# A decoder layer on one core: in cross attention ScalarE copies first and VectorE scales the normalised rows; in the experts VectorE makes the down weights' low parts

## What is computed

```python
x = _layernorm(x + attn(x))                        # 16 heads, decayed linear attention
x = _layernorm(x + xattn(x, ctx_1024, ctx_1024))   # 16 heads of 16, 77 keys per sequence, softmax
# experts: xf is x as 4096 rows
probs = softmax(xf @ router_w.T); keep the top 2 and renormalise
g = xf @ gate_w[e] + gate_b[e]; u = xf @ up_w[e] + up_b[e]
expert_out = (silu(g) * u) @ down_w[e] + down_b[e]
y = sum_e probs[e] * expert_out[e]
x = _layernorm(x + y)
```

## Time and profile before

| | |
|---|---|
| median of 3 runs | 1626.9 us (1623.96 to 1629.72) |
| profiled execution | 1613.4 us, span 1611.6 us |
| TensorE busy | 1337.4 us (83%) |
| VectorE, ScalarE, GpSimd busy | 52%, 55%, 50% |
| granted clock of TensorE | 0.917 in the mean |

### The profile page before, as it was taken

One profiled execution on the slowest core, in us unless ns is written; L12 is line 12 of the kernel. 1 busy time (PEld: TensorE's weight loads), 2 busy tenths in 40 slices (PEclk: granted clock), 3 DMA queues, 4 the chain that ended last, 5 costly groups with the idle time before them and its releaser, 6 DMA issues. The chain is left out here.

```text
span 1611.6 us, 30998 instructions
## 1 busy us (share of the span) xinstructions
PE 1337.4 (83%) x10439; PEld 1125.3 (70%) x10439; DVE 841.4 (52%) x1783; ACT 892.4 (55%) x2002; POOL 808.8 (50%) x847
## 2 busy tenths in 40 slices
PE   5999999999999999996877777842699999998500
PEld 4788888888888888885655555522588888888500
DVE  3344444544444444452666566549445544556466
ACT  4677777777777777774255556520345544555200
POOL 2244444444444444454466767611475666667375
PEclk9999999999999999998899999965699999999755
DMA  3300000000000000001223223202254454456154
GB/s 124 74 14 21 21 14 21 21 21 21 15 21 21 21 14 21 15 15 36 69 57 94 75 69 100 63 27 82 72 186 151 143 166 157 153 171 177 52 147 143
DMA packets 123556, 116.42 MB, mean 72 GB/s; under 512 B 42242, under 2 KB 104298, under 8 KB 123434
## 3 DMA queue, kind: packets, MB, share of 16 engines
q1 hardware_dynamic: 116618, 96.23, 19.3%
q0 software_dynamic: 6816, 18.62, 4.3%
HBM read 83.93 MB, written 24.07 MB: 67 GB/s over the span
## 5 line engine op out<-in xcount | busy, mean ns | idle before, releaser
L290 POOL TENSOR_SCALAR_AFFINE_SELECT a_decay<-a_decay 128x256 f32<-128x256 f32 x256 | 113.7, 448 | 260.5 <-ACT a_decay L370 260.5
L493 DVE TENSOR_TENSOR a_probs<-a_ps_s,a_decay 128x384 f32<-128x384 f32 x256 | 131.5, 552 | 164.6 <-PE a_ps_o L668 152.9
L299 POOL TENSOR_TENSOR a_key_sum<-a_probs 128x256 f32<-128x256 f32 x128 | 94.5, 738 | 170.2 <-DVE a_probs L493 159.1
L333 ACT ACTIVATE a_qk_exp<-a_ps_qk 128x512 f32<-128x512 f32 x128 | 76.5, 598 | 136.7 <-PE a_ps_qk L574 129.7
L574 PE MATMUL a_ps_qk<-a_xT_hi,a_w_hi 128*128 128x256 f32 x512 | 144.6, 282 | 3.6 <-ACT a_qk_relu L334 3.6
L486 DVE SCALAR_TENSOR_TENSOR a_qk<-a_qk_exp,a_qk_relu 128x512 f32<-128x512 f32 x128 | 89.3, 698 | 106.9 <-ACT a_qk_relu L334 106.9
L574 PE MATMUL a_ps_qk<-a_xT_lo,a_w_hi 128*128 128x256 f32 x512 | 143.5, 280 | 0.0
L574 PE MATMUL a_ps_qk<-a_xT_hi,a_w_lo 128*128 128x256 f32 x512 | 143.4, 280 | 0.0
L649 PE MATMUL a_ps_s<-a_qk 64*128 64x256 f32 (+1 forms) x1024 | 132.2, 338 | 0.6 <-DVE a_probs L493 0.2
L368 ACT ACTIVATE a_decay<-a_ps_c,a_c_now 128x256 f32<-128x256 f32 x256 | 124.4, 486 | 2.3 <-PE a_ps_c L639 1.4
L956 POOL TENSOR_TENSOR b_probs<-b_probs,b_top 128x1232 f32<-128x1232 f32 x32 | 72.6, 2270 | 103.6 <-DVE b_top L1124 103.6
(11 more groups left out here) (283 smaller groups left out, 4129.4 us busy)
## 6 DMA issues: line engine op xcount, KB each, us to landing
e_gu_raw<-in_L_ffn_gate_w SPq DMA_DIRECT2D x23, 512.0 KB, 3.7
e_gu_raw<-in_L_ffn_up_w SPq DMA_DIRECT2D x23, 512.0 KB, 5.2
e_dn_raw<-in_L_ffn_down_w SPq DMA_DIRECT2D x23, 512.0 KB, 6.7
y_sorted<-e_y_out SPq DMA_DIRECT2D x16, 512.0 KB, 2.9
a_x_in<-in_x SPq DMA_DIRECT2D x16, 256.0 KB, 2.7
a_x_res<-in_x SPq DMA_DIRECT2D x16, 256.0 KB, 2.7
x_rows<-a_x SPq DMA_DIRECT2D x16, 256.0 KB, 2.1
b_x_in<-x_rows SPq DMA_DIRECT2D x16, 256.0 KB
```

The costliest lines, as they stand in the source:

```text
L290: pool.affine_select(out=d, in_=d, compare_op=ALU.is_ge, fill=0.0, base=0, pattern=[[0, 2], [1, P]], channel_multiplier=-1)\
L299: pool.tensor_tensor(key_sum[:], probs[:, :, P:N], probs[:, :, N:TRI], ALU.add).then_inc(keys_summed, 1)
L333: act.activation(qk_exp[:], ps_qk[:], ACT.Exp)
L493: vec.tensor_tensor(probs[:, h, :], ps_s[h][:, 0:TRI], decay[h][:], ALU.mult)\
```

## The change

In `cross_attention`, ScalarE's `normalise` is split. ScalarE keeps only the inverse root (`root`), two small instructions, and has them behind the copies of `pT` and of the queries instead of ahead of them. VectorE gets `scale_x2`, which subtracts the mean and multiplies in one instruction per block, between the maximum of the next sequence's first scores and the sums of the second block. The negative root and the shift are dropped. In `run_experts` the down weights' low part goes from GpSimd to VectorE (`dn_low`), to the end of VectorE's tile, and once ahead of the first tile.

```diff
--- before.py
+++ after.py
@@ -782,7 +782,6 @@
         resid = sb("b_resid", [P, NB, D])
         stats, mv = sb("b_stats", [P, NB, 6]), sb("b_mv", [P, NB, 2])
         ln_var, rstd = sb("b_ln_var", [P, NB]), sb("b_rstd", [P, NB])
-        minus_rstd, shift = sb("b_minus_rstd", [P, NB]), sb("b_shift", [P, NB])
         x2, x2T = sb("b_x2", [P, NB, D]), sb("b_x2T", [P, KC, N])
         v_dram = nc.dram_tensor("b_v_scratch", [ROWS, D], F32).ap()
 
@@ -1024,26 +1023,14 @@
                     act.wait_ge(y_made, b)
                 act.copy(oT[:], ps_o[:]).then_inc(oT_kept, 1)
 
-            def normalise(b):
+            def root(b):
 
                 act.wait_ge(var_ready, b + 1)
                 act.activation(ln_var[:], mv[:, :, 1], ACT.Ln, bias=eps_col[:]).then_inc(rstd_step, 1)
-                act.wait_ge(rstd_step, 4 * b + 1)
+                act.wait_ge(rstd_step, 2 * b + 1)
+                if has(b, -1):
+                    act.wait_ge(x2_ready, b)
                 act.activation(rstd[:], ln_var[:], ACT.Exp, scale=-0.5).then_inc(rstd_step, 1)
-                act.wait_ge(rstd_step, 4 * b + 2)
-                act.activation(minus_rstd[:], rstd[:], ACT.Copy, scale=-1.0).then_inc(rstd_step, 1)
-                act.wait_ge(rstd_step, 4 * b + 3)
-                for blk in range(NB):
-                    ins = act.activation(shift[:, blk:blk + 1], mv[:, blk, 0:1], ACT.Copy, scale=minus_rstd[:, blk:blk + 1])
-                ins.then_inc(rstd_step, 1)
-                act.wait_ge(rstd_step, 4 * b + 4)
-                if has(b, -1):
-                    act.wait_ge(x2_stored, 32 * b)
-                    act.wait_ge(x2T_made, b)
-                for blk in range(NB):
-                    ins = act.activation(x2[:, blk, :], resid[:, blk, :], ACT.Identity, bias=shift[:, blk:blk + 1],
-                                         scale=rstd[:, blk:blk + 1])
-                ins.then_inc(x2_ready, 1)
 
             def keep_x2T(b):
                 act.wait_ge(x2T_made, b + 1)
@@ -1054,12 +1041,12 @@
             def sequence(b, par, turn):
                 if has(b, 1):
                     keep_xT(b + 1)
-                if has(b, -2):
-                    normalise(b - 2)
                 if has(b, -1):
                     keep_pT(b - 1, 1 - par, 1)
                 if has(b, 1):
                     keep_q(b + 1)
+                if has(b, -2):
+                    root(b - 2)
                 if has(b, -1):
                     keep_oT(b - 1)
                 exponentials(b, par, 1)
@@ -1080,9 +1067,9 @@
             all_sequences(act, sequence)
             keep_pT(B - 1, (B - 1) % 2, 1)
             keep_oT(B - 1)
-            normalise(B - 2)
+            root(B - 2)
             keep_x2T(B - 2)
-            normalise(B - 1)
+            root(B - 1)
             keep_x2T(B - 1)
 
         @block.vector
@@ -1147,6 +1134,16 @@
                     ins = vec.bn_aggr(mv[:, blk, :], stats[:, blk, :])
                 ins.then_inc(var_ready, 1)
 
+            def scale_x2(b):
+                vec.wait_ge(rstd_step, 2 * b + 2)
+                if has(b, -1):
+                    vec.wait_ge(x2_stored, 32 * b)
+                    vec.wait_ge(x2T_made, b)
+                for blk in range(NB):
+                    ins = vec.tensor_scalar(x2[:, blk, :], resid[:, blk, :], mv[:, blk, 0:1], rstd[:, blk:blk + 1],
+                                            ALU.subtract, ALU.mult)
+                ins.then_inc(x2_ready, 1)
+
             def keep_logits(b):
                 vec.wait_ge(lg_made, b + 1)
                 vec.tensor_copy(logits_all[:, bass.ts(b, NB), :], ps_lg).then_inc(lg_kept, 1)
@@ -1156,6 +1153,8 @@
                 sums(b, par, 0)
                 if has(b, 1):
                     keep_scores(b + 1, 1 - par, 0)
+                if has(b, -2):
+                    scale_x2(b - 2)
                 sums(b, par, 1)
                 if has(b, -1):
                     add_residual(b - 1)
@@ -1172,8 +1171,10 @@
                 for t in range(KC):
                     keep_k(c, t)
             all_sequences(vec, sequence)
+            scale_x2(B - 2)
             add_residual(B - 1)
             statistics(B - 1)
+            scale_x2(B - 1)
             keep_logits(B - 2)
             keep_logits(B - 1)
 
@@ -1644,6 +1645,7 @@
 
         rows_loaded, table_turned, table_ready = sem("e_rows_loaded"), sem("e_table_turned"), sem("e_table_ready")
         where_loaded, sp_turns, pool_turns = sem("e_where_loaded"), sem("e_sp_turns"), sem("e_pool_turns")
+        vec_turns = sem("e_vec_turns")
         w_loaded, b_loaded = sems("e_w_loaded"), sems("e_b_loaded")
         x_loaded, y_stored = sems("e_x_loaded"), sems("e_y_stored")
         counts_ready, count_step = sem("e_counts_ready"), sem("e_count_step")
@@ -1750,10 +1752,6 @@
                 pool.sem_inc(pool_turns, 1)
                 pool.tensor_tensor(gu_lo[par][:], gu_raw[par][:], gu_hi[par][:].bitcast(F32), ALU.subtract)\
                     .then_inc(gu_lo_done[par], 1)
-                pool.wait_ge(dn_hi_done[par], turn + 1)
-                pool.sem_inc(pool_turns, 1)
-                pool.tensor_tensor(dn_lo[par][:], dn_raw[par][:], dn_hi[par][:].bitcast(F32), ALU.subtract)\
-                    .then_inc(dn_lo_done[par], 1)
 
             def tile(t, par, turn):
                 if has(t, 1):
@@ -1839,6 +1837,12 @@
                     vec.wait_ge(y_made[n], rounds(t) + blk // 2 + 1)
                     vec.tensor_tensor(y_out[par][:, blk, :], ps_y[n][:, 0:D], dn_bias[par][:], ALU.add).then_inc(y_kept[n], 1)
 
+            def dn_low(par, turn):
+                vec.wait_ge(dn_hi_done[par], turn + 1)
+                vec.sem_inc(vec_turns, 1)
+                vec.tensor_tensor(dn_lo[par][:], dn_raw[par][:], dn_hi[par][:].bitcast(F32), ALU.subtract)\
+                    .then_inc(dn_lo_done[par], 1)
+
             def tile_index(t, par):
                 if has(t, -2):
                     vec.wait_ge(x_turned, t - 1)
@@ -1873,6 +1877,8 @@
                 for f in range(2, FC):
                     hidden(f)
                     hid_low(f)
+                if has(t, 1):
+                    dn_low(1 - par, turn + par)
 
             vec.wait_ge(counts_ready, 2)
             vec.tensor_copy(count[:], count_i[:]).then_inc(count_step, 1)
@@ -1895,6 +1901,7 @@
             tile_index(0, 0)
             tile_index(1, 1)
             x_low(0, 0)
+            dn_low(0, 0)
             all_tiles(vec, tile)
             keep_y(TILES - 1, (TILES - 1) % 2, (TILES - 1) // 2)
 
```

## The result

The changed kernel takes 1631.2 us in the median of 8 runs (1630.3 to 1632.8), the kernel before, in 8 runs too, 1625.0 (1621.8 to 1629.7). The ratio is 1.0036 (95% interval 1.0022 to 1.0051): some 6 us slower.

What follows compares the result with a forecast made beforehand. Cross attention was taken as a loop through all engines, TensorE as bound in 512-row tiles, VectorE held by GpSimd in 256-row tiles. Terms +3.9 - 2.1 - 1.3 - 0.5 = 0.0 us gave 1627 us, range 1612 to 1638.

Steps and rivals of the forecast that it cites:

- the likeliest case: Whole kernel: the forecast of no net change, about 1627 us, own range 1619 to 1635, chance 0.58.
- GpSimd between the scalings: Cross attention: GpSimd's subtraction gets in between VectorE's two scalings, so the sums start 2.7 us later per sequence.
- Rival (a): Cross attention: VectorE does both scalings ahead of GpSimd's subtraction; -1.65 us per sequence, 1602 us in all; chance 0.12.
- The copy comes 2.4 us earlier: Cross attention: ScalarE copies `pT` 3.2 us after VectorE's reciprocal instead of 5.6, saving 2.4 us per sequence.
- The clock: Cross attention: TensorE's granted clock may fall to 1.2 GHz at its wait for x2; only a rival, not in the sum.
- rival (c): Cross attention: TensorE's x2 wait lowers its clock, 2.0 us per sequence in half of twelve; 1637 us; chance 0.23.
- The cross term: Cross attention: +2.7 - 2.4 = +0.3 us per sequence, times 13 sequences, +3.9 us.
- The end effect: Cross attention: the last sequence and the two normalisations after the loop, under 1 us, left out of the sum.
- The experts' start: Start of the experts: VectorE's selectors are delayed less without GpSimd's down low part there; -2.1 us.
- Tiles of 512: Expert tiles of 512 rows: GpSimd gathers earlier, TensorE's waits for gathered rows may go; 0 to -2.1, taken -1.3 us.
- Tiles of 256: Expert tiles of 256 rows: VectorE's gain turns into a wait for weights; -0.5 us over six tiles, bounds -9.5 and +3.
- The bound without late weights: Expert tiles of 256 rows: if weights are never late, 10.3 us per tile, -9.5 us.

Runs made afterwards that it cites:

- one_and_one: Changed kernel, but one of VectorE's two scalings comes ahead of the next first scores, the other stays behind their maximum; ratio 0.9812 to the kernel before.
- tensor_filler: Changed kernel, but TensorE makes each sequence's output projection twice to fill its wait for x2; ratio 0.9969 to the kernel before.

## Why the prediction was right, and where it was not

The measured time, 1631.2, lies in the stated range (1612 to 1638) and in the likeliest case's own (1619 to 1635), but by 0.36% (0.22 to 0.51) the change falls at the edge of "within 0.3%", to which I gave 0.47; slower had 0.26. The forecast was no change, the measured one is +6.3 us, and it was that near by luck, because errors cancel: each part alone, cross attention came out 11.9 us worse than forecast (15.8 for 3.9) and the experts 5.2 us better (-9.1 for -3.9).

- **GpSimd between the scalings** (2.7 us per sequence): right. 2.5 us, in every turn; one_and_one shows that it needs two instructions in a row. Rival (a) is out. Together with the next point the order costs 0.2 us per turn at full clock, where I had 0.3.
- **The copy comes 2.4 us earlier**: right in tensor_filler, where the copy follows in 3.2 us and the turn is 17.0; in the changed kernel 1.5 us, as TensorE turned x at half the clock.
- **The clock**: this step failed. The sum puts it at nothing; I had it only as rival (c), with 0.23, in half of the sequences at 2.0 us each. It fell in all of them, at 1.3 us each in the mean. "There TensorE's wait for `pT` goes, and was as long" was no reason against it: the new wait is 2.3 us long in every turn, behind the output projection and ahead of light work. The cross term was +3.9 and measured +16.8 in the profile, of which the turns give 12 x 1.38 = 16.6. The end effect that I left out gives back 2.4 (from the thirteenth logits to the last), and the first sequences, ahead of the first logits, cost 2.6 more.
- **The experts' start**: -2.1 forecast, -2.1 measured, the slow batch 6.23 us where I said 6.2. (My own shares give 2.2, rounded down.)
- **Tiles of 512**: -1.3 forecast. -2.9 measured, but 2.3 and 2.5 of such a gain stand in profiles without the edit, so the edit's own part may be near nothing.
- **Tiles of 256**: -0.5 forecast, -5.1 measured. The mechanism was right (the waits for weights, the chain over SP: 3.27 and 1.0 us, as in the earlier trace rows); two sizes were off. (The bound without late weights is -9.8 by my own 10.3 and 11.93, not -9.5.) The down weights landed 1475.89 - 1469.72 = 6.2 us after their issue and not 7.5, and a tile without a wait takes 10.13 and not 10.3. Over three pairs that is 3 x 1.3 + 3 x 0.17 = 4.4 us of the 4.6 that were missed.

## What to carry to other kernels

What a reordering gives should be priced with TensorE's next wait: a new wait of 2.3 us cost 1.3 us more per turn here through the granted clock behind it, and work of no use put into the wait was a gain of 11 us. Where VectorE must work beside GpSimd, a single instruction that starts first slips in ahead, and two in a row let GpSimd's waiting one come between; the simplest answer here, and as good as any, was to leave the work where it was and only change its order. And a wait on two results ahead of a load of both should be taken apart as soon as the two are made by different engines.

## What the runs showed of the hardware

VectorE's reduction with one input isn't held by GpSimd: in one_and_one it takes 1.43 us beside the subtraction, and all 32 of the changed kernel, beside GpSimd or not, take 1.42 to 1.44; `scalar_tensor_tensor` with two inputs in SBUF is held like `tensor_scalar` (2.49 and 2.36 us at most, 0.48 and 0.41 in the median). The last stage takes 94 us on one chip and 107 to 111 on two others, for one and the same code, which moves a whole profile by 0.8%; profiles should be compared stage by stage.
